# One program for the three stages of a conditioned sequence network: the weight fold moved to the head, the core fed by rank, FFN jobs put among the core's first and last super block

## The reference

```python
def ffn(role, x, W_down, b_down, W_up, b_up, gamma, beta):      # layers 0, 2, 3
    h = gelu(x @ W_down[role] + b_down[role])                    # 512 -> 256
    y = x + h @ W_up[role] + b_up[role]                          # 256 -> 512
    return layernorm(y) * gamma[role] + beta[role]

def core(x, codes, ...):                                         # layer 1
    attn = softmax((x @ Wq) @ (x @ Wk).T * 512 ** -0.5)
    a = attn @ (x @ Wv) @ Wp + bp
    cms = gelu(a @ cW1 + cb1) @ cW2 + cb2 + one_hot(codes, 512)
    mod = gelu(concat(a, cms) @ mW1 + mb1) @ mW2 + mb2           # hidden size 2048
    return clip(x + cms + mod, 0, 1)
```

## Time and profile before

| | us |
|---|---|
| median of 3 runs (2557.7 to 2562.58) | 2557.92 |
| the profiled execution, own time | 2554.5 |
| its span, first to last instruction | 2552.4 |
| PE busy | 2457.7 |
| DVE, ACT, POOL busy | 1022.9, 901.2, 401.4 |
| DMA, mean | 76 GB/s |

### The profile page before, as it was taken

One profiled execution on the slowest core, in us unless ns is written; L12 is line 12 of the kernel. 1 busy time (PEld: TensorE's weight loads), 2 busy tenths in 40 slices (PEclk: granted clock), 3 DMA queues, 4 the chain that ended last, 5 costly groups with the idle time before them and its releaser, 6 DMA issues. The chain is left out here.

```text
span 2552.4 us, 27604 instructions
## 1 busy us (share of the span) xinstructions
PE 2457.7 (96%) x11376; PEld 2043.5 (80%) x11376; DVE 1022.9 (40%) x1399; ACT 901.2 (35%) x1227; POOL 401.4 (16%) x310
## 2 busy tenths in 40 slices
PE   5998999999999999999999999999999999879995
PEld 4876888888888888888888888888888888668884
DVE  4763333422233334223243432233334222268775
ACT  3643333322324322223243322233423222156663
POOL 2781000000000000000000000001000000038887
PEclk9998999999999999999999999999999999989997
DMA  5553111121120112111211121111111110164243
GB/s 190 207 173 132 50 50 50 42 75 41 42 100 34 50 50 83 50 50 39 77 50 50 50 83 48 40 46 67 50 50 50 50 50 17 42 215 142 74 140 132
DMA packets 41297, 193.24 MB, mean 76 GB/s; under 512 B 5699, under 2 KB 5699, under 8 KB 24789
## 3 DMA queue, kind: packets, MB, share of 16 engines
q1 hardware_dynamic: 35412, 149.54, 17.1%
q0 software_dynamic: 5760, 41.95, 4.2%
HBM read 160.01 MB, written 31.46 MB: 75 GB/s over the span
## 5 line engine op out<-in xcount | busy, mean ns | idle before, releaser
L1174 DVE TENSOR_TENSOR h_lo<-g,h_hi 128x512 fp32r<-128x512 f32 x256 | 179.7, 702 | 752.4 <-ACT h_hi L1072 752.0
L1070 ACT ACTIVATE g<-bank,bias_cols 128x512 f32<-128x512 f32 x256 | 176.6, 690 | 655.5 <-PE bank L59 419.7
L57 PE MATMUL bank<-h_hi,w_hiB 128*128 128x512 f32 x1024 | 398.9, 390 | 0.0
L59 PE MATMUL bank<-h_hi,w_loB 128*128 128x512 f32 x1024 | 398.5, 389 | 0.0
L58 PE MATMUL bank<-h_lo,w_hiB 128*128 128x512 f32 x1024 | 398.5, 389 | 0.0
L57 PE MATMUL bank<-o_hi,w_hiA 128*128 128x512 f32 x768 | 299.2, 390 | 0.0
L59 PE MATMUL bank<-o_hi,w_loA 128*128 128x512 f32 x768 | 298.8, 389 | 0.0
L58 PE MATMUL bank<-o_lo,w_hiA 128*128 128x512 f32 x768 | 298.8, 389 | 0.0
L1030 ACT ACTIVATE w_hiB<-w_raw 128x2048 fp32r<-128x2048 f32 x36 | 69.1, 1919 | 523.4 <-PE bank L59 523.4
L1253 POOL COPY acc<-xr 128x1024 f32<-128x1024 f32 x16 | 15.9, 1034 | 1365.2 <-PE bank L984 1349.7
L59 PEld LDWEIGHTS bank<-h_hi,w_loB 128*128 128x128 f32 x1024 | 192.2, 188 | 39.8
(11 more groups left out here) (216 smaller groups left out, 4392.6 us busy)
## 6 DMA issues: line engine op xcount, KB each, us to landing
w_raw<-in_units_a SPq DMA_DIRECT2D x32, 1024.0 KB, 4.9
w_raw<-in_units_b SPq DMA_DIRECT2D x32, 1024.0 KB, 4.8
w_raw<-in_w_packed SPq DMA_DIRECT2D x30, 512.0 KB, 4.1
w_raw<-in_units_c SPq DMA_DIRECT2D x15, 1024.0 KB, 4.8
w_raw<-in_rows_packed SPq DMA_DIRECT2D x20, 512.0 KB, 4.6
x_tok<-x SPq DMA_DIRECT2D x16, 512.0 KB, 7.3
x<-stage SPq DMA_DIRECT2D x32, 256.0 KB, 2.2
first_gain<-in_rows_packed SPq DMA_DIRECT2D x10, 512.0 KB, 4.9
```

The costliest lines, as they stand in the source:

```text
L57: pe.matmul(out, lh, rh, start=(i == 0), stop=False)
L59: last = pe.matmul(out, ll, rh, start=False, stop=(i == len(terms) - 1))
L1070: act.activation(g[q % 2][:], bank[q % 4][:], ACT.Gelu, bias=bias_at).then_inc(gelu_done, 1)
L1174: v.tensor_tensor(h_lo[:, j, cols(n)], g[q % 2][:], h_hi[:, j, cols(n)].bitcast(F32), ALU.subtract).then_inc(hlo_done, 1)
```

## The change

Route, first FFN, core and last FFN become one program (`program`) without barriers. The classes `Route` and `Ffn` hold the same steps as before as methods, one per engine, and each engine's queue is one list. What is computed stays the same.

- Head: SP loads roles, the first two factors of the fold, then the codes, then the rest. Routing on DVE is written anew (49 small steps, the first gather after 30); it waits for the codes before it reads the roles. PE does the first half of the fold (`fold(0)`) right after routing, then transposes(0), two tiles of the second half, down(0), transposes(1), the last two tiles. The folded weights go to scratch from two tiles of `x` instead of from `w_raw`.
- The rows that the first FFN scatters are ordered by rank (sequences sorted by role, without padding), so super block 0 needs groups 0 to 3 alone. The target codes are put in that order by a product on PE.
- The first FFN's scatters count on five semaphores by group, `STORES = (0, 0, 0, 0, 1, 1, 2, 3, 4, 4)`, so that SP's load of super block s waits for its groups alone. The gather that reuses a tile waits on the first of them.
- PE goes from down(9) to the core's transposes with the up tiles of jobs 8 and 9 between them. ACT waits for the first two store semaphores ahead of its first core copy; POOL keeps gain, shift and scatter of groups 7 to 9, waits for their scatters and then copies x into `acc`. The first unit for slot C is loaded during chunk 0.
- `attend` waits for value tiles one by one.
- End of super block 3: transposes(0) of the last FFN follow out tile 0, finish is put between out tiles and the halves of down(0), and up(0), down(1), transposes(2) follow closer. The last FFN's gathers of groups 0 to 5 read super blocks 0 to 2, and wait for their stores only.
- Tail: DVE does gain and shift of half of job 17 and of all of 18 and 19.

PE from super block 3 into the last FFN, before: the end of the last output tile (`w_hiB`, `w_loB` are its weights), the finish, the block's start and job 0.

```diff
+    def pool_gather(self, pool, j, ready, rows=NROWS):
+        if j >= 2:
+            pool.wait_ge(self.tr_done, 2 * (j - 2) + 2)
+        if j >= self.NX:
+            pool.wait_ge(self.stored[0], 16 * (j - self.NX + 2))
...
+    def sp_load_gain(self, sp, j):
+        if self.NL > 1 and j == self.NJ - 1:
+            sp.wait_ge(self.add_done, 2 * (j - 2) + 1)
+            sp.wait_ge(self.last_add, self.HALF)
+        elif j >= 2:
+            sp.wait_ge(self.add_done, 2 * (j - 2) + 2)
...
+    STORES = (0, 0, 0, 0, 1, 1, 2, 3, 4, 4)
@@ SP @@
+            def load_x(s, to):
+                for i in ((0,), (1,), (2, 3), (4,))[s]:
+                    sp.wait_ge(first.stored[i], 16 * STORES.count(i))
...
+            sp.dma_start(routed.role_i[:], roles).then_inc(routed.role_in, 16)
+            for to, of, loaded in loads[0:2]:
+                sp.dma_start(to, of).then_inc(loaded, 16)
+            sp.dma_start(routed.codes_i[:], codes.rearrange("a n -> n a")).then_inc(routed.codes_in, 16)
+            sp.dma_start(routed.cb2_sb[:], cb2).then_inc(routed.cb2_in, 16)
+            for to, of, loaded in loads[2:4]:
+                sp.dma_start(to, of).then_inc(loaded, 16)
...
+                if j == NG - 2:
+                    load_x(0, x_first)
+                    sp.wait_ge(first.wdlo_done, NG - 1)
+                    sp.wait_ge(fold_stored[0], 16)
+                    sp.dma_start(w_raw[0], fold_m).then_inc(raw_in[0], 16)
+            sp.wait_ge(first.wdlo_done, NG)
+            sp.wait_ge(fold_stored[1], 16)
+            sp.dma_start(w_raw[1], fold_v).then_inc(raw_in[1], 16)
...
+                    if s == 0 and c == 0:
+                        load_bc(s, 2, 0, units_c[0])
@@ PE @@
-                pe.wait_ge(v_done, TT * s + TT)
                 for k in range(KD):
+                    if n == 0:
+                        pe.wait_ge(v_done, TT * s + HT + k + 1)
...
+            routed.pe_tables(pe)
+            fold(0, range(KD))
+            pe.wait_ge(routed.dve, routed.ALL)
+            first.pe_transposes(pe, 0)
+            fold(1, range(2))
...
+            transposes(0, range(4))
+            first.pe_up(pe, NG - 2, range(1, GT), role)
+            transposes(0, range(4, TT))
+            first.pe_up(pe, NG - 1, range(GT), first.role_of(pe, NG - 1))
             query(0, 0)
...
+            pe.wait_ge(gelu_done, HIDDEN)
+            last.pe_transposes(pe, 0)
+            out_tiles(SB - 1, 2 * CH - 1, range(1, 6))
+            finish(SB - 1, range(4))
+            out_tiles(SB - 1, 2 * CH - 1, range(6, TILES))
+            pe.wait_ge(acc_done, HIDDEN - 2)
+            last.pe_down(pe, 0, range(1))
+            finish(SB - 1, range(4, TT))
+            last.pe_down(pe, 0, range(1, KB))
+            pe.wait_ge(fin_done, TT * SB)
+            last.pe_transposes(pe, 1)
+            role = last.role_of(pe, 0)
+            last.pe_up(pe, 0, range(2), role)
+            last.pe_down(pe, 1)
+            last.pe_up(pe, 0, range(2, 3), role)
+            last.pe_transposes(pe, 2)
+            last.pe_up(pe, 0, range(3, GT), role)
@@ ACT @@
+            for i in (0, 1):
+                act.wait_ge(first.stored[i], 16 * STORES.count(i))
+            transposed(0, range(4))
+            first.act_norm(act, NG - 3, range(HALF))
+            split("A", 1)
+            transposed(0, range(4, TT))
+            first.act_norm(act, NG - 3, range(HALF, GT))
+            first.act_moments(act, NG - 2)
+            act.wait_ge(first.up_done, GT * NG)
+            split("B", 1)
+            queried(0, 0)
+            first.act_norm(act, NG - 2, range(GT))
+            first.act_moments(act, NG - 1)
+            act.wait_ge(first.stored[2], 16 * STORES.count(2))
@@ DVE @@
+        v.wait_ge(self.made, 12)
+        v.wait_ge(self.codes_in, 16)
+        step(v.tensor_copy(self.codes_f[:], self.codes_i[:]))
+        v.wait_ge(self.role_in, 16)
+        step(v.tensor_copy(self.role_f[:], self.role_i[:]))
...
+            last.dve_gain_shift(v, j - 2, range(HALF, GT), 0)
+            last.dve_gain_shift(v, j - 1, range(GT), HALF)
+            last.dve_gain_shift(v, j, range(GT), HALF + GT)
@@ POOL @@
+            for j in range(NG - 2, NG):
+                first.pool_gain_shift(pool, j)
+                first.pool_scatter(pool, j)
+            for i in (3, 4):
+                pool.wait_ge(first.stored[i], 16 * STORES.count(i))
             for s in range(SB):
                 pool.wait_ge(xraw_done, TT * s + TT)
```

1562 lines of the change are left out of this document (896 added, 666 removed).

## The result

The changed kernel takes 2517.81 us (median of 4 runs, 2516.26 to 2519.3) against 2560.25 (2557.7 to 2562.64) for the kernel before beside it: ratio 0.9834, interval 0.9822 to 0.9847, 42.4 us faster. The profiled execution has a span of 2516.0 against 2552.4, 36.4 less, and an own time of 2517.75. Forecast were 2507.2 for the span and 2512 for the median. The direction and the size are right, and the time lies in the range of the forecast's own case; the terms of the sum are not all right.

The account below looks back on a forecast made before the run. PE bounds the kernel, busy 2457.7 of 2552.4 us, so only idle and half-speed time can be won: 2552.4 - 10.0 - 1.4 - 27.0 - 6.8 = 2507.2 span, plus 2.1 and 3.4 gives median 2512; range 2489 to 2524.

Parts of the forecast that it names:

- the forecast's own case: Whole kernel: the forecast of 2512 us with its own range 2503 to 2521, chance 0.58.
- Head: Program start: codes land near 10.1 behind two weight loads, fold starts near 18.3, down(1) at 56.5 against 45.69.
- That small loads might overtake: Head: if small loads overtake the 1 MB weight loads, the fold's start is 4.5 us earlier.
- POOL's stop: First FFN: gathers of groups 7, 8, 9 each wait for a full scatter landing of 7.5; POOL loses 18.4 us.
- The step that failed: First FFN's end: PE waits 6.8 us for gather 9's rows, covered by ACT's longer wait for scatter 5, landing at 196.1.
- From scatter 5 to the query: First FFN to core: scatter 5 lands at 196.1, the first query starts at 209.8; 10.0 us won up to there.
- Attend: Core's four blocks: waiting tile by tile wins 4 x 0.34 = 1.4 us.
- Rival B: Core's first block: POOL's two rounds after moments(9) miss the attend; at its bound 10 us, 2523; chance 0.11.
- Core to last FFN: Join of core and last FFN: down(2) starts at 2246.9 instead of 2273.9, 27.0 us won; bounds 14 and 28.4.
- Rival C: Join with the last FFN gets only half, 14 us instead of 27, giving 2526; chance 0.07.
- Tail: End of last FFN: DVE multiplies and adds straight on, last scatter at 2539.0, 6.8 us won; bounds 0 and 8.
- Rivals A and D: A: landings take 4.5, 29.6 won at first seam, 2493, chance 0.2; D: core's blocks at 1.2 GHz, 2560 us, chance 0.03.

Follow-up runs that it names:

- own semaphores: Changed kernel with groups 0 to 3 counting scatters on four semaphores, so gathers 7, 8, 9 wait for groups 0, 1, 2 alone; 2494.16 us, ratio 0.9747.
- the shorter ACT wait alone: Changed kernel, shared semaphore kept, ACT's wait before its first core copy leaving out scatter 5; 2513.35 us.
- The norm put behind the split: Changed kernel with ACT, in jobs 5 to 7, splitting the next job's tokens before the norm that waits for POOL; 2515.8 us, ratio 0.9832.
- the kernel before with the added wait: Kernel before, gathers of groups 7 to 9 also waiting for the scatter just ahead of them; 2583.41 us against 2557.43, ratio 1.0100.
- with the rstd first: Changed kernel with POOL doing the older job's rstd and shift before the gather in rounds gathering groups 7 to 9; 2510.35 us.
- with the join undone: Changed kernel with PE doing all output tiles and the whole finish of super block 3 before the last FFN's transposes(0) and down(0); 2524.54 us.
- with the scatters alone: Changed kernel with gain and shift loads of jobs 2 to 5 held until the scatter two jobs before has landed; 2507.63 us.

## Why the prediction was right, and where it was not

**Head.** Right in kind: the codes land behind the factors at 10.12 (10.1 forecast). The fold starts at 19.36 instead of 18.3, since the steps and the turns through PE cost 1.1 more. That small loads might overtake is out. From the fold's start to transposes(2) the sum has 45.4 us (down(1) at 56.5 and 7.2 more); 46.1 were measured here and 45.0 to 46.0 in the other executions.

**POOL's stop.** The mechanism was right: three gathers wait for a full landing. The size was low, 18.4 us: from scatter 1 to scatter 4 POOL takes 176.60 - 113.90 = 62.7 where it had 142.89 - 102.23 = 40.7, 22.0 lost. Landings were 7.5, 8.6 and 8.5 where I took 7.5 for each, and each gather leaves some 0.8 us after the landing, for which I had nothing. Scatter 5 leaves at 188.91 instead of 184.7. The end of the old stretch, in the kernel before:

```profile
142.89 1.05 POOL L676 DMA_INDIRECT x<-first_x,first_dst_row  x1 [0.29 <-POOL first_x L653]
```

**The step that failed** is "Gather 9 then leaves at 160.0 ...; PE wants it at 158.6 and waits 6.8", with the sentence that the wait for scatter 5 covers it. I followed only the instruction that waits, and who wants its result. I did not read what stands behind it: rstd_shift(j-2) on POOL, norm(j-2) on ACT, which waits for it, and behind that the split of the next job. That way PE is held in each of the three rounds, 21.1 us by transposes(9), three times my figure, over a quarter of it by the clock, for which I had nothing there. So PE brings the core's first tile at about 195, and ACT waits for scatter 5 only 4.25 us, not some 13; the 10 us for which PE was to idle before the core's second four transposes are not there either, its waits in that place are 1.58 and 0.98. The experiments bear this out: own semaphores give 23 us, the shorter ACT wait alone 4.5. The norm put behind the split shows the wait that I named, hidden behind the one that I missed.

That the number still came out near is partly luck. The query's time hung on the landing of scatter 5, a term that I had nearly right, and PE's hold, which I had 14 us too small, stayed just under it: without that landing the query comes only 4.5 us earlier.

**From scatter 5 to the query** I counted 13.7 us (196.1 to 209.8); it took 17.9 (199.43 to 217.34). I had put the last tiles of up(8) ahead of the wait, but DVE's residuals for them (it adds the FFN's input) are queued behind its subtractions of the core's tiles, which wait for ACT; the row at 201.88 shows PE waiting 1.58 us for such a residual. The scatter left 4.2 later and landed a little faster (10.4 against 11.4), which makes 3.3, and 4.2 more here: the 7.5 us by which the term was off.

**Attend.** 1.4 forecast for the four blocks, 2.3 measured, 0.57 a block where I had 0.34: the printed wait is not all of it. Rival B stayed out by less than I had: POOL's copies began at 265.15 and ended at 269.14, and ACT, which is the one to wait for them, was free for its next step at 269.91. That is a slack of 0.8 us, where I had 3.5.

**Core to last FFN.** 27.0 forecast, 26.5 measured; from the last gelu to down(2) 49.2 and 49.66. DVE was late twice, as worked out: 0.57 at the first up tile, by the second hidden subtraction (0.4 forecast), and 1.03 (1.0). Rival C is out.

**Tail.** The last scatter 6.8 earlier, measured 6.9; the 1.6 us behind it were not in the sum.

**Sum.** The span came out 8.8 us above the forecast, 7.6 of it at the first seam and 1.6 at the end. The median is only 5.8 above, because I added 3.4 for the distance of the runs of before from their profiled one; this kernel's median lies within 0.1 of its profiled run. That step had no ground beyond one execution, and that it took back some 3 us of the miss is luck. Rivals A and D are out as well: landings beside a gain load are long, and inside the core's blocks, where PE never waits long, the granted clock of the changed kernel reads 1.00 from 220 to 2480 in every window of 20 us.

## What to carry to other kernels

If several transfers are counted on one semaphore and a wait asks, as here, for all of them issued so far, a wait for an older one becomes a wait for the newest: give the one that is reused early a semaphore of its own. When a wait is added, follow the queue behind the waiting instruction, and the queue behind everyone who waits for that, before asking who wants the waiting instruction's own result. Idle stretches of a busy PE can also have a price behind them, by the clock: three waits in a row cost two fifths as much again in the changed kernel and a half in the kernel before with the added wait.

## What was not expected of the hardware

In the first FFN a 1 MB indirect scatter lands in 4.5 to 5.2 us alone and, in the changed kernel, in 7.4 to 8.6 with one 0.5 MB broadcast load started beside it, whose own landing is 4.4 to 5.6. The load that costs this was issued by the same event that released the scatter; to put it behind the landing was worth 10 to 12 us here.

PE waits of 3.9 us and more in the first FFN were each followed by 3 to 6 us at the 1.2 GHz level. Shorter ones do not foretell it: behind 2.53 us (with the rstd first) and 1.67 us (with the join undone) the level was there for 3.4 us, behind 1.95 us (with the rstd first), and even behind 3.68 us (with the scatters alone), it was not. The same instructions with the same wait of 3.04 us lost 2.6 us more by transposes(2) in one execution than in another.
